# Attention before a mixture-of-experts block on one core: TensorE's order within a slot drawn anew, and a part of the statistics on another engine

## The reference, cut to what matters

```python
x = x + _layernorm(_L0_attn_ref(_layernorm(x), keys, values, ...))   # 16 heads of 8
x = x + _layernorm(_L0_ffn_ref(_layernorm(x), ...))                  # 4 heads of 32, then 8 experts
# the first attention, q, k, v each behind a relu:
score = jnp.einsum('bhsd,bhtd->bhst', qh, kh) / jnp.sqrt(jnp.float32(DH))
attn = jax.nn.softmax(score, axis=-1)
a = jnp.einsum('bhst,bhtd->bhsd', attn, vh)
a = jnp.transpose(a, (0, 1, 3, 2)).reshape(q.shape[0], q.shape[1], q.shape[2])
```

## Time and profile before

| | us |
|---|---|
| three timed runs | 609.35, 609.4, 610.09 |
| median | 609.4 |
| profiled execution, device time | 609.53 |
| its span in the trace | 607.8 |
| copy of slot 0's values (L1646), first of 32 | 82.3 |
| copy of slot 31's, last of 32 | 396.4 |

### The profile page before, as it was taken

One profiled execution on the slowest core, in us unless ns is written; L12 is line 12 of the kernel. 1 busy time (PEld: TensorE's weight loads), 2 busy tenths in 40 slices (PEclk: granted clock), 3 DMA queues, 4 the chain that ended last, 5 costly groups with the idle time before them and its releaser, 6 DMA issues.

```text
span 607.8 us, 9821 instructions
## 1 busy us (share of the span) xinstructions
PE 510.6 (84%) x3475; PEld 198.5 (33%) x3475; DVE 521.4 (86%) x853; ACT 407.3 (67%) x837; POOL 194.2 (32%) x309
## 2 busy tenths in 40 slices
PE   1887899999999999999999999967857898978910
PEld 1544122222222222222222222346645765533300
DVE  5979889999999999999999998255998768799986
ACT  1752589898989888889888988824546330233963
POOL 7000112049504534133470317528357530000000
PEclk9979599999999999999999999998989899999965
DMA  8945011010221112111012200011000000000112
GB/s 226 302 139 143 20 28 37 23 42 26 74 64 37 31 33 57 51 58 41 23 34 69 72 21 12 7 51 35 1 2 1 1 1 1 1 0 0 36 35 69
DMA packets 31792, 28.93 MB, mean 48 GB/s; under 512 B 6256, under 2 KB 23800, under 8 KB 31744
## 3 DMA queue, kind: packets, MB, share of 16 engines
q1 hardware_dynamic: 29712, 27.33, 15.8%
q10 hardware_dynamic: 2032, 0.98, 0.6%
HBM read 19.23 MB, written 8.65 MB: 46 GB/s over the span
## 4 chain that ended last, share of the span: by engine, by line
PE 44%; DVE 32%; POOL 9%; ACT 7%; issue 5%; DMA 2%; SPq 0%; ACTq 0%; DVEq 0%
PE ps L1518 13%; PE ps L1513 10%; DVE row_max L1704 9%; PE ps L1486 5%; DVE space L940 4%; PE ps L585 2%; DVE space L876 2%; ACT space L829 2%; ACT attended L1646 2%; POOL space L402 2%; POOL space L404 2%; POOL smallp L399 1%; DVE st L234 1%; PE ps L609 1%; PE ps L592 1%
## 5 line engine op out<-in xcount | busy, mean ns | idle before, releaser
L1704 DVE TENSOR_REDUCE row_max<-ps 128x2 f32<-128x1024 f32 x256 | 299.7, 1219 | 17.4 <-PE ps L1486 14.4
L1630 ACT ACTIVATE space<-ps 128x512 f32<-128x512 f32 x512 | 272.7, 605 | 44.0 <-PE ps L1513 43.4
L1513 PE MATMUL ps<-space 51*128 51x512 bf16 x512 | 157.8, 389 | 3.4 <-DMA space<-max_turned 2.6
L1518 PE MATMUL ps<-space 128*32 128x512 f32 x1024 | 138.1, 612 | 2.1
L1486 PE MATMUL ps<-space 48*128 48x512 bf16 x512 | 126.4, 394 | 8.6 <-DVE row_max L1704 7.0
L1513 PEld LDWEIGHTS ps<-space 51*128 51x128 bf16 x512 | 40.7, 94 | 162.3 <-ACT space L1630 143.0
L1361 POOL CAST max_parts<-row_max 128x16 bf16<-128x16 f32 x32 | 6.3, 197 | 232.9 <-DVE row_max L1704 232.8
L585 PE MATMUL ps<-W,space 128*128 128x512 f32 x128 | 65.4, 592 | 0.0
L940 DVE TENSOR_REDUCE space<-ps 128x128 f32<-128x1024 f32 x32 | 38.6, 1218 | 9.0 <-PE ps L585 8.8
L448 POOL TENSOR_TENSOR space<-PC,same_row 128x512 f32<-128x512 f32 x32 | 33.0, 1061 | 32.6 <-DVE PC L890 24.5
L1486 PEld LDWEIGHTS ps<-space 48*128 48x128 bf16 x512 | 26.3, 94 | 50.0 <-DVE row_max L1704 42.4
(11 more groups left out here) (233 smaller groups left out, 636.9 us busy)
## 6 DMA issues: line engine op xcount, KB each, us to landing
space<-q_parts_dram SPq DMA_DIRECT2D x64, 48.0 KB
attended_dram<-attended SPq DMA_DIRECT2D x128, 18.0 KB
X<-in_L_attn_queries SPq DMA_DIRECT2D x8, 256.0 KB, 7.7
space<-in_L_ffn_w SPq DMA_DIRECT2D x2, 1024.0 KB, 6.2
space<-q_parts_dram SPq DMA_DIRECT2D x64, 32.0 KB
space<-attended_dram SPq DMA_DIRECT2D x16, 128.0 KB, 2.4
space<-inverses_dram SPq DMA_DIRECT2D x16, 128.0 KB
out<-space SPq DMA_DIRECT2D x4, 512.0 KB, 3.2
```

The costliest lines, as they stand in the source:

```text
L1513: pe.matmul(ps[:, col_bank(v), :], k_rows[rows_a, kappa // 4 % 2, tc * P:(tc + 1) * P], q_stack[rows_a, kappa % 4, b * S:(b + 1) * S], sta ...
L1518: mm = pe.matmul(ps[32 * m:32 * m + 32, PV, :], v_heads[:, tc, PAIR * (kappa // 4) + m % PAIR, :], probs[:, tc % 2, m, :], start=(tc == 0) ...
L1630: act.activation(probs[:, tc % 2, m, :], ps[:, col_bank(v), :], ACT.Exp, scale=1.0 / math.sqrt(DH)).then_inc(s_pr, 1)
L1704: dve.tensor_reduce(row_max[:, par].rearrange("p (a c) -> p a c", a=PAIR)[:, :, item], ring(n), AX.X, MAX).then_inc(s_free, 1)
```

## The change

- TensorE: `step` is replaced by `slot`, which is one list for a whole slot, and two lists for the last two slots. The last column product of a slot's first `tc` moves ahead of the slot. Products with v for `tc` 1 and 2 are done in two halves of 256 columns each; those for `tc` 0 and 3 stay whole. The turn stands behind the first product with v. In the last slot two pieces of the first group (6 and 7) move behind the last product with v.
- `probs` has three buffers in place of two.
- ScalarE: the turned maxima are copied ahead of the last exponential of `tc` 1 (before: behind it).
- SP: the shift DMAs come ahead of the stores, with a semaphore for each of the two; the denominators are loaded alone in slot c = 1 of the next eight and behind the slot's own DMAs, the attended values in c = 2, the inverses in c = 3.
- VectorE: `dve_invert` moves from c = 1 to c = 2. Its statistics stay for group 2 alone: those of `A` in slot 29, those of `X` within `first_group_copies`.
- GpSimd: for groups 0 and 1 it makes mean and variance itself (`pool_centre`, `pool_variance`, `pool_scale`): a sum over 128 features by halves, seven additions from 512 elements per partition down to 8, twice for each norm. A group's work is spread over slots c = 4 to 10.

```diff
+        probs = [view(space4, 0, [QB, S]), view(space4, QB * S, [QB, S]), view(space8, 0, [QB, S])]
         ET = view(space4, 0, [QPG, 16, P])
...
+        s_split, s_shift = sem("max_split"), [sem(f"shift_loaded{a}") for a in range(PAIR)]
         s_sc, s_pr = sem("columns_scored"), sem("probs_ready")
...
+        def pool_add_up(pool, ch, src, scratch, total):
+            n = D // 2
+            ch.done(pool.tensor_tensor(scratch[:, :, 0:n], src[:, :, 0:n], src[:, :, n:2 * n], ADD))
+            ch.wait()
+            while n > 2:
+                n //= 2
+                ch.done(pool.tensor_tensor(scratch[:, :, 0:n], scratch[:, :, 0:n], scratch[:, :, n:2 * n], ADD))
+                ch.wait()
+            ch.done(pool.tensor_tensor(total.rearrange("p (b o) -> p b o", o=1), scratch[:, :, 0:1],
+                                       scratch[:, :, 1:2], ADD))
+            ch.wait()
...
+        def pool_centre(pool, ch, src, dst, scratch):
+            mean = smallp[:, 0, :]
+            pool_add_up(pool, ch, src, scratch, mean)
+            ch.done(pool.tensor_scalar(mean, mean, 1.0 / D, None, MUL))
+            ch.wait()
+            ch.done(pool.tensor_tensor(dst, src, over_f(mean), SUB))
+            ch.wait()
...
+        def pool_variance(pool, ch, dst, scratch):
+            var = smallp[:, 2, :]
+            ch.done(pool.tensor_tensor(scratch, dst, dst, MUL))
+            ch.wait()
+            pool_add_up(pool, ch, scratch, scratch, var)
+            ch.done(pool.tensor_scalar(var, var, 1.0 / D, EPS, MUL, ADD))
+            ch.wait()
...
+        def pool_scale(pool, ch, dst):
+            var, inv = smallp[:, 2, :], smallp[:, 3, :]
+            ch.done(pool.tensor_tensor(inv, var, neg_half[:], ALU.pow))
+            ch.wait()
+            return pool.tensor_tensor(dst, dst, over_f(inv), MUL)
...
-            pool.wait_ge(s_st, 2 * g + 1)
-            ch.done(pool_norm(pool, ch, A[:, g], A[:, g]))
-            ch.wait()
...
+            scratch = XN[:, g]
+            if c == 4:
+                pool_divide(pool, ch, g)
+            if g < G - 2:
+                if c == 5:
+                    pool.wait_ge(s_r1, g + 1)
+                    pool_centre(pool, ch, A[:, g], A[:, g], scratch)
+                if c == 6:
+                    pool_variance(pool, ch, A[:, g], scratch)
+                if c == 7:
+                    ch.done(pool_scale(pool, ch, A[:, g]))
+                    ch.wait()
+                    pool_residual(pool, ch, g)
+                if c == 8:
+                    pool.wait_ge(s_r2, g + 1)
+                    pool_centre(pool, ch, X[:, g], A[:, g], scratch)
+                if c == 9:
+                    pool_variance(pool, ch, A[:, g], scratch)
+                if c == 10:
+                    pool_scale(pool, ch, A[:, g]).then_inc(s_n2, 1)
+                    pool_out_bias(pool, g)
+            else:
+                if c == 6:
+                    pool.wait_ge(s_st, 1)
+                    ch.done(pool_norm(pool, ch, A[:, g], A[:, g]))
+                    ch.wait()
+                    pool_residual(pool, ch, g)
+                if c == 7:
+                    pool.wait_ge(s_st, 2)
+                    pool_norm(pool, ch, X[:, g], A[:, g]).then_inc(s_n2, 1)
+                    pool_out_bias(pool, g)
...
-        def dve_statistics(dve, ready, g, src, tc):
-            if tc == 0:
-                dve.wait_ge(ready, g + 1)
-            for b in (2 * tc, 2 * tc + 1):
-                ins = dve.bn_stats(st6p[:, b, :], src[:, g, b, :])
-            if tc == TC - 1:
-                ins.then_inc(s_st, 1)
+        def dve_statistics(dve, bs, src):
+            for b in bs:
+                ins = dve.bn_stats(st6p[:, b, :], src[:, G - 2, b, :])
+            return ins
...
+                if kappa + 1 < NQ:
+                    sp.wait_ge(s_pr, turn_item(kappa + 1) + 1)
+                    load_shift(kappa + 1)
                 if kappa:
                     sp.wait_ge(s_pve, kappa)
                     store_attended(kappa - 1)
-                if kappa + 1 < NQ:
-                    sp.wait_ge(s_pr, turn_item(kappa + 1) + 1)
-                    load_shift(kappa + 1)
...
+                slot(kappa)
                 if c == 1 and g:
+                    load_denominators(g - 1)
+                if c == 2 and g:
                     load_attended(g - 1)
-                if c == 2 and g:
                     store_inverses(g - 1)
                 if c == 3 and g:
                     load_inverses(g - 1)
-                slot(kappa)
...
+            load_denominators(G - 1)
             load_attended(G - 1)
...
+                if g >= 2:
+                    pool_group(pool, ch, g - 2, c + 8)
                 if g:
-                    if c == 3:
-                        pool_divide(pool, ch, g - 1)
-                    if c == 5:
-                        pool_residual(pool, ch, g - 1)
-                    if c == 7:
-                        pool_input(pool, ch, g - 1)
+                    pool_group(pool, ch, g - 1, c)
...
-                if tc == 0 and m == 0:
-                    pe.wait_ge(s_shift, 32 * (kappa + 1))
+                if tc == 0 and m < PAIR:
+                    pe.wait_ge(s_shift[m], 16 * (kappa + 1))
...
+            def multiply_v(kappa, tc, half=None):
+                cols = slice(0, S) if half is None else slice(half * S // 2, (half + 1) * S // 2)
+                if not half:
+                    if tc == 0 and kappa:
+                        pe.wait_ge(s_pve, kappa)
+                    pe.wait_ge(s_pr, column_item(kappa, tc, QB - 1) + 1)
                 for m in range(QB):
-                    mm = pe.matmul(ps[32 * m:32 * m + 32, PV, :], v_heads[:, tc, PAIR * (kappa // 4) + m % PAIR, :],
-                                   probs[:, tc % 2, m, :], start=(tc == 0), stop=(tc == TC - 1))
-                if tc == TC - 1:
+                    mm = pe.matmul(ps[32 * m:32 * m + 32, PV, cols], v_heads[:, tc, PAIR * (kappa // 4) + m % PAIR, :],
+                                   probs[(TC * kappa + tc) % 3][:, m, cols], start=(tc == 0), stop=(tc == TC - 1))
+                if tc == TC - 1 and half != 0:
                     mm.then_inc(s_pv, 1)
...
+            score_columns(0, 0, QB - 1)
+            def slot(kappa):
...
+                row(0)
+                for m in range(3):
+                    column(1, m)
+                row(1)
+                multiply_v(kappa, 0)
+                turn_max(kappa + 1)
+                column(1, 3)
...
+                multiply_v(kappa, 1, 0)
...
+            def last_slot(kappa):
...
+                multiply_v(kappa, 2)
+                multiply_v(kappa, 3)
+                first_group(pe, 6)
+                first_group(pe, 7)
...
-            for kappa in range(NQ):
-                for tc in range(1, TC):
-                    exps(kappa, tc)
-                    if tc == 1 and kappa + 1 < NQ:
-                        copy_turned(kappa + 1)
-                if kappa + 1 < NQ:
-                    exps(kappa + 1, 0)
+            def copy_attended(kappa):
                 act.wait_ge(s_pv, kappa + 1)
                 if kappa >= 2:
                     act.wait_ge(s_ast[kappa % 2], 64 * (kappa // 2))
                 act.copy(attended[:, kappa % 2, :], ps[:, PV, :]).then_inc(s_pve, 1)
+            copy_turned(0)
+            for kappa in range(NQ):
+                exps(kappa, 0)
+                if kappa:
+                    copy_attended(kappa - 1)
+                exps(kappa, 1, range(0, 3))
+                if kappa + 1 < NQ:
+                    copy_turned(kappa + 1)
+                exps(kappa, 1, range(3, QB))
+                exps(kappa, 2)
+                exps(kappa, 3)
+            copy_attended(NQ - 1)
...
+                    if j == 1:
+                        dve.wait_ge(s_r2, G - 1)
+                        dve_statistics(dve, range(B), X).then_inc(s_st, 1)
...
-                    if g and c == 1 and tc == 2:
+                    if g and c == 2 and tc == 2:
                         dve_invert(dve, g - 1)
-                    if g and c == 4:
-                        dve_statistics(dve, s_r1, g - 1, A, tc)
-                    if g and c == 6:
-                        dve_statistics(dve, s_r2, g - 1, X, tc)
+                    if g == G - 1 and c == 5:
+                        if tc == 0:
+                            dve.wait_ge(s_r1, G - 1)
+                        ins = dve_statistics(dve, (2 * tc, 2 * tc + 1), A)
+                        if tc == TC - 1:
+                            ins.then_inc(s_st, 1)
                 slot(kappa, between)
             first_group_copies()
```

128 lines of the change are left out of this document (83 added, 45 removed).

## The result

| | before | after |
|---|---|---|
| median of the runs, us | 609.38 (608.59 to 610.09, 4 runs) | 583.83 (583.33 to 585.64, 4 runs) |
| profiled execution, us | 609.5 | 585.64 |
| its span, us | 607.8 | 583.9 |
| ratio after / before | | 0.9579, 95% interval 0.9559 to 0.9599 |

A forecast was written before the change was run, and what follows sets the result against it. The prediction took a ring through three banks, column 3 behind the product with v, to bound the slot. Slots 2 to 29 -20.9, slots 0 and 1 -1.5, last two -1.1, behind them -0.5: 609.5 to 585.5 us, range 581.5 to 593.

The forecast's parts named there:

- the ring: Slots before: a loop through three banks, column 3 waiting behind the product with v, 2.39 us a step, bounds the slot.
- The new slot, 9.23: Slots 2 to 29: walking TensorE's new list with row prices gives 9.23 us per slot against 9.94.
- The changes of form: TensorE going between column or row products and products with v: 0.09 to 0.10 us each, thirteen a slot, 1.2.
- rival 1: Slots: changes of form hide, TensorE needs 7.6, VectorE alone sets 9.13 per slot; 582.7, at best 581.5; 8%.
- Rival 2: Slots: TensorE's waits don't overlap; a reduction in a full stretch goes at 1.17, giving 9.4 per slot; 590 to 595; 20%.
- Rival 4: Half products with v: halving doesn't halve; a run of 0.36 gives 10.2 per slot and 609; 3%.
- it fits, with 1.5 us to spare: SP's shift DMAs in the new slot: landed at 4.5 and 5.3 us, needed at 6.59.
- Three inversions, 0.85 each: VectorE in slots 2 to 29: three inversions of 0.95, with 0.1 to spare per slot, cost 2.5 us.
- GpSimd's slot 6, +1.0: Slot 6: two copies take 9.4 with the split's 1.05 on top, so split and turn come late: +1.0 us, once.
- Ahead of slot 1, -0.8: Slot 0 and ahead of it: the order begins alike at half the clock, given a gain of 0.8 us.
- Slots 30 and 31, -1.1: Last two slots: pieces 6 and 7 move behind and their two changes of form go; 19.7 us against 20.80.
- Behind slot 31, -0.5: Behind slot 31's copy: denominators loaded first, so the second maxima start at 9.9 against 10.4 us: -0.5.

The follow-up runs named there:

- old_order: The kernel after, with TensorE's order of before in slots 0 to 29 and ScalarE's copy of the turned maxima placed accordingly: 602.86 us, ratio 0.989.
- whole: The kernel after, with the products with v of tc 1 and 2 whole, at the place of their first halves: 595.04 us, ratio 0.9772.
- short_max: c_spread with VectorE's maxima over 256 of the 512 columns of each half of the scores: a single run of 577.38 us.
- c_spread: The kernel after, with its 16 c_rows loads spread behind slots 2 to 8 and GpSimd's work on them moved later: 581.67 us, ratio 0.9549.
- together: c_spread with both of GpSimd's c_stack copies in slot 9 and two selects each in slots 10 and 11: 582.92 us, ratio 0.9555.
- pool_longer: c_spread with further GpSimd multiplications, meant for twelve slots of its sums but also run in others, which changes the output: 608.64 us, ratio 0.9981.
- pieces_back: c_spread with pieces 6 and 7 of the first group back between slot 31's products with v: 581.08 us, ratio 0.9525.
- stats_dve: The kernel after, with the statistics of groups 0 and 1 on VectorE again and the norm on GpSimd in one piece: 595.09 us, ratio 0.9765.
- dens_mixed: c_spread with the last group's attended and denominator loads in turn, in place of the denominators first: 583.23 us, ratio 0.956.
- k_behind_shift: The kernel after, with SP's two loads of the next k rows behind the slot's shift in place of ahead of it: 589.01 us, ratio 0.966.
- copies_apart: The kernel after, with GpSimd's two c_stack copies one each in slots 6 and 7, selects in 8 and 9: 586.12 us, ratio 0.9626.

## Why the forecast held, point by point

- **What bounded before, and the ring.** With before's order alone the slot is 9.94 again (old_order), although VectorE, GpSimd and SP are relieved as in after: TensorE's order set the pace, as forecast. That the ring goes through the three banks is read from the rows; no run changed their number. And the forecast gave no shares: the order alone is worth 0.15 of the 0.67 per slot, the halves 0.52 (whole).
- **The new slot, 9.23.** Measured 9.27, place by place as walked. The price of a half product, 0.57 to the next column, and of the changes of form, 0.09 to 0.10, are those taken from the earlier trace rows. The forecast called TensorE the bound with VectorE right behind. short_max shows that VectorE isn't the bound: it could be twice as fast for nothing. That it is TensorE and not its ring with ScalarE is argued from the walk.
- **The changes of form, and rival 1.** The column at 219.34 is followed by the product at 219.65, 0.09 over the 0.22 that a column holds its half, and with VectorE relieved (short_max) the slot does not fall under 9.27. Rival 1 is out. The Trainium skill ("TensorE: Matmul & The Clock Gate", section "Architectural detail: the array is 16× 32×32, not 1× 128×128") says that weight loads can be pulled ahead of matmuls in flight, by which these changes would be free; the row goes against it.
- **Rival 2's 1.17 and rival 4's sum.** A full stretch of reductions goes at 1.156, between the forecast's 1.14 and the rival's 1.17, and ends at 9.25 per slot. Rival 4 has a slip in its sum: a run of 0.36 makes 10.2 per slot, and 585.5 + 28 x 0.97 is 612.7, not 609.
- **The shift, "it fits, with 1.5 us to spare", and SP, "late by 0.4 to 1.4, within its slack".** Here the forecast failed. It summed SP's slot from the group's loads and left out `load_c`, whose four loads (2.99 us) stand behind each of slots 2 to 5. 3.05 for shift and stores, 3.79 for the stack and 3.0 for `c_rows`, with the gaps, are 10.03 in a slot of 9.27, so the queue falls 0.8 behind in each; in slot 5 k rows (1.55) come on top. The shift's issue at 122.97 is 6.3 behind the slot's copy, where it is 2.5 in an ordinary slot of c_spread. TensorE waits for 1.9 of these 3.8, so the slack was there as forecast; what the sum had too low was the queue's load. c_spread takes the cause away and 5.2 us with it; the sign "no wait of TensorE for the shift" was the one that failed. At 9.94 per slot the same queue had been nearly level: the faster slot made SP a bound.
- **Three inversions, 0.85 each.** 0.60 each (9.87 against 9.27). They show one interval later than the slot numbers given, 11, 19 and 27. So VectorE had some 0.35 to give each time where it was given 0.1: 9.27 less 9.13 is 0.14, and the rest may be what its two buffers hold (not tested).
- **Slot 29, 0.55.** 0.48.
- **GpSimd's slot 6, +1.0.** Not there in after (interval 7 is 9.27), since TensorE was late already; 0.84 where it is not late (together). GpSimd's variance slot takes 6.2 against 6.4, and the 8.2 that a slot covers is right for slots in a row (pool_longer).
- **Slots 2 to 29.** 262.5 forecast, 267.0 measured, 261.75 in c_spread: the term that was put at nothing is SP's. The rest is small and cancels in part: 28 slots at 9.27 are 1.1 over, the copies' 1.0 and 0.8 of the inversions and the statistics did not come.
- **Ahead of slot 1, -0.8.** -2.7: mis-sized. Full clock comes back earlier: the windows of 73 to 79 us have 0.60 in before and 0.91 in after, 0.97 in whole and 0.64 in old_order, with TensorE busy for 5.9 to 6.0 of the 6 in each. So it hangs on TensorE's new order, halves or not; all traces with it have the first copy at 78.0 to 80.5, the two without it at 82.0 and 82.3. Why this order brings the clock back sooner stays open.
- **Slots 30 and 31, -1.1.** -1.12. But the reason given (pieces 6 and 7 and their changes of form) is a displacement: put back they cost 1.93 here and give back 2.14 behind (pieces_back). The step was one sum in two terms.
- **Behind slot 31, -0.5.** -3.0, and for another reason. The inversion starts 8.81 behind the copy (9.49 before), as worked out, but that lead is spent by 14 us behind it: the subtraction that follows takes 0.97, beside GpSimd's multiplications, where it takes 0.29 in before. So the term forecast is 0.0. The terms left out are the half clock at 411 us that after no longer has (1.6) and the later one (1.4), which belongs to no edit.
- **Statistics.** Freeing VectorE was priced; that the norm in one piece would be too long for GpSimd in a 9.27 slot was not. In stats_dve that is four times 1.35 of some 10.6 in the slots of the groups, and 1.5 more for the clock in one of them.

So the point forecast was right by its main term and by two misses of opposite sign, +4.5 (slots 2 to 29, by SP's queue) and -4.4 (mainly the clock, ahead of slot 1 and behind slot 31), of about the same size. Nothing ties the two together: that they cancel is luck. By the first alone it would have been 590, by the second alone 581.

## What to carry to other kernels

When a slot gets shorter, sum every queue against the new length, the DMA-issuing one too and in every slot, one-time loads included: a queue that is level at 9.94 loses 0.8 each time at 9.27, and nothing shows until its slack is gone. A late queue costs more than the wait that shows: waits of 1.9 us of TensorE cost 5.2 with the fall of the clock behind them, and waits of 1.15 still cost 3.0 at full clock (stats_dve). And engines at 97% don't say which of them binds: make one of them faster in an experiment and see whether the slot moves.

## What the runs showed of the chip

- Work of an unchanged tail of 200 us varies by 3 us with where one fall of TensorE's clock lands: 208.3 to 211.3 in kernels with the same instructions there.
- A power on GpSimd goes by the element: 20.76 us for 128, where a product of 128 takes 0.40, and 1.67 for 8, where a product takes 0.20.
- SP's issue of one transfer, 0.3 to 0.8 us as a rule, now and then takes 1.1 to 1.8 (in after a load of k rows, in dens_mixed a store, in k_behind_shift a load of attended values), and with little slack the shift is late for it. That this is a source of the runs' scatter is likely, but not shown.
- TensorE's clock fell to half behind some waits of 1.0 to 1.5 us and not behind others: behind 1.0 in pool_longer (0.54 in the window of 247 to 250.7), 1.27 in stats_dve at 296.6, 1.31 in copies_apart and 1.49 in after, but not behind 1.28 in stats_dve at 237.8 and 318.2, nor behind 1.49 in dens_mixed at 191.25 (1.00 in each). The length of the wait alone doesn't decide it.
- VectorE's reductions from PSUM are not slowed by a GpSimd that is busy for 90% of the time (1219 ns against 1217), while its short subtraction of two SBUF tiles in after takes 0.29 with GpSimd idle and 0.97 beside GpSimd's multiplications of SBUF tiles (L516, 384.49 to 388.60), ending just behind them:

```profile
382.84 0.29 DVE L949 TENSOR_TENSOR space<-space,mx 128x128 f32<-128x128 f32 x1
...
387.78 0.97 DVE L949 TENSOR_TENSOR space<-space,mx 128x128 f32<-128x128 f32 x1
```

The Trainium skill ("SBUF — State Buffer", section "Who interferes with whom") says that a VectorE instruction with two inputs from SBUF contends with a GpSimd instruction that reads SBUF, and one with at most one does not. These rows agree with both halves of it.
